# Adding the causal mask on VectorE inside the maximum instead of on TensorE, in a two-layer transformer kernel

## What is computed

```
scores = q @ k.T * scale                     # 1024 x 1024 for each of 16 heads
scores[query, key] = -inf  where key > query # causal
probs  = softmax(scores)                     # subtracts the maximum of each query's row
y      = probs @ v
```

## Time and profile before

| | |
|---|---|
| median of 3 runs | 812.42 us |
| the three runs | 810.61, 815.0, 812.42 us |
| span of the profiled execution | 814.8 us (the only time listed for that execution; it is 0.2 us under the slowest of the three) |
| attention of layer 0, maxima and scores | about 36 to 180 us of the span |
| attention of layer 1, maxima and scores | about 463 to 607 us |

### The profile page before, as it was taken

One profiled execution on the slowest core, in us unless ns is written; L12 is line 12 of the kernel. 1 busy time (PEld: TensorE's weight loads), 2 busy tenths in 40 slices (PEclk: granted clock), 3 DMA queues, 4 the chain that ended last, 5 costly groups with the idle time before them and its releaser, 6 DMA issues.

```text
span 814.8 us, 13117 instructions
## 1 busy us (share of the span) xinstructions
PE 667.2 (82%) x4319; PEld 434.2 (53%) x4319; DVE 475.5 (58%) x1293; ACT 331.5 (41%) x693; POOL 241.8 (30%) x276
## 2 busy tenths in 40 slices
PE   3979999993878999999506879999982999999960
PEld 2534344332547999999404424334331646899950
DVE  4498788427773344444395798778317662234457
ACT  3554566672233333222124444576763231333301
POOL 2140101210026775444300470101210003477620
PEclk9998999997689999999856989999997599999995
DMA  3442210320139999998340533030006100299662
GB/s 93 142 134 88 73 33 1 121 87 1 52 118 300 315 315 305 310 303 287 132 140 1 155 118 104 3 109 2 2 2 219 62 0 27 88 285 310 214 206 72
DMA packets 60325, 108.52 MB, mean 133 GB/s; under 512 B 11237, under 2 KB 37179, under 8 KB 60132
## 3 DMA queue, kind: packets, MB, share of 16 engines
q1 hardware_dynamic: 52564, 93.86, 35.9%
q0 software_dynamic: 7632, 13.80, 5.3%
q10 hardware_dynamic: 64, 0.03, 0.0%
HBM read 79.98 MB, written 19.79 MB: 122 GB/s over the span
## 4 chain that ended last, share of the span: by engine, by line
PE 62%; DVE 24%; ACT 4%; DMA 4%; issue 3%; SPq 1%; POOL 1%; ACTq 0%; POOLq 0%; DVEq 0%
PE ps L1023 15%; DVE mx L1411 9%; PE ps L838 7%; PE ps L822 6%; PE ps L793 5%; PE ps L911 5%; PE ps L1036 5%; PE ps L1038 5%; DVE X L1720 3%; PE ps L753 2%; PE ps L737 2%; ACT X L1164 2%; PE ps L880 2%; PE ps L997 2%; PE ps L982 1%
## 5 line engine op out<-in xcount | busy, mean ns | idle before, releaser
L1411 DVE TENSOR_REDUCE mx<-ps 128x1 f32<-128x512 f32 (+3 forms) x304 | 180.3, 656 | 44.4 <-PE ps L796 37.3
L1164 ACT ACTIVATE X<-ps 128x1024 f32<-128x1024 f32 (+1 forms) x192 | 146.3, 810 | 78.0 <-PE ps L822 77.4
L793 PE MATMUL ps<-KA,QA 112*128 112x512 bf16 (+3 forms) x384 | 113.2, 344 | 8.1 <-DMA KA<-X 2.7
L702 POOL DMA_INDIRECT outs<-X,token x95 | 94.9, 999 | 72.8 <-DVE X L1698 56.3
L694 POOL DMA_INDIRECT V<-token_rows,row_of_slot x64 | 65.4, 1021 | 123.7 <-DVE row_of_slot L1595 63.2
L672 POOL TENSOR_SCALAR_AFFINE_SELECT X<-X 128x512 f32<-128x512 f32 x64 | 40.8, 638 | 203.1 <-ACT X L1164 203.1
L1023 PE MATMUL ps<-QA,KA 128*128 x756 | 95.2, 276 | 4.5 <-ACT QA L1256 3.7
L822 PE MATMUL ps<-QA,KA 114*128 114x512 bf16 (+3 forms) x384 | 93.2, 329 | 4.5 <-ACT X L1164 3.4
L1023 PEld LDWEIGHTS ps<-QA,KA 128*128 128x128 f32 x756 | 91.9, 192 | 7.5 <-issue 5.6
L1685 DVE TENSOR_TENSOR X<-ps,X 128x128 f32<-128x128 f32 x95 | 27.7, 292 | 106.7 <-ACT X L1267 106.5
L838 PE MATMUL ps<-X,V 128*32 128x512 f32 (+3 forms) x768 | 81.1, 497 | 0.5 <-ACT X L1172 0.4
(11 more groups left out here) (255 smaller groups left out, 892.3 us busy)
## 6 DMA issues: line engine op xcount, KB each, us to landing
KA<-in_ex SPq DMA_DIRECT2D x95, 512.0 KB
X<-in_dn SPq DMA_DIRECT2D x95, 64.0 KB
outs<-empty SPq DMA_DIRECT2D x4, 1024.0 KB, 8.5
X<-outs SPq DMA_DIRECT2D x8, 512.0 KB, 6.3
V<-outs SPq DMA_DIRECT2D x8, 512.0 KB, 7.8
QA<-X SPq DMA_DIRECT2D x28, 128.0 KB, 2.4
KA<-X SPq DMA_DIRECT2D x28, 128.0 KB, 2.5
QA<-w_sdn SPq DMA_DIRECT2D x28, 128.0 KB, 2.5
```

The costliest lines, as they stand in the source:

```text
L702: pool.indirect_dma_start(out=outs[L], out_offset=bass.IndirectOffsetOnAxis(ap=token[L][:, i:i + 1], axis=0), in_=erows[:, g % OUT_RING, : ...
L793: mm = pe.matmul(ps[:, bank, j * w:(j + 1) * w], QA[0:KQ, h, i * P:(i + 1) * P], KA[0:KQ, h, s0:s0 + w], start=True, stop=not diag)
L1164: nc.scalar.activation(probs[:, st % PB, 2 * p:2 * p + 2, off:CH], ps[:, 4 + 2 * p:6 + 2 * p, off:CH], ACT.Exp, scale=SCALE).then_inc(S(f" ...
L1411: v.tensor_reduce(mx[:, part, i, h0:h0 + nh], ps[:, n % RB, 0:nh * w].rearrange("p (h w) -> p h w", h=nh), AX.X, ALU.max)\
```

## The change

In units that hold one head and lie on the diagonal, TensorE no longer adds the mask. VectorE takes the maximum there with another instruction: it adds a mask row to the bank, element by element, writes the sums back over the bank, and gives the largest of them, at least -1e30, to `mx`. The mask becomes 512 columns wide (`mask_row`), 0 except for its last 128 columns, which are the former `mask_q`; the instruction takes its last 384 or 512 columns. Units with two or four heads a bank keep their matmul with the mask and their reduction. The order of the work and the semaphores stay.

```diff
-        mask_q = sb("mask_q", [P, P], BF16)
+        mask_row = sb("mask_row", [P, CH], BF16)
+        mask_q = mask_row[:, CH - P:CH]
...
-            for t in (identf, identb, mask_q):
+            for t in (identf, identb, mask_row):
                 ch.step(pool.memset(t[:, :], 0.0))
...
-            ch.step(pool.affine_select(out=mask_q[:, :], in_=mask_q[:, :], compare_op=ALU.is_ge, fill=-BIG,
+            ch.step(pool.affine_select(out=mask_q, in_=mask_q, compare_op=ALU.is_ge, fill=-BIG,
                                        base=0, pattern=[[-1, P]], channel_multiplier=1))
...
                             h = HG * g + h0 + j
-                            diag = s0 + w == (i + 1) * P
+                            diag = s0 + w == (i + 1) * P and nh > 1
                             mm = pe.matmul(ps[:, bank, j * w:(j + 1) * w], QA[0:KQ, h, i * P:(i + 1) * P],
                                            KA[0:KQ, h, s0:s0 + w], start=True, stop=not diag)
                             if diag:
-                                mm = pe.matmul(ps[:, bank, (j + 1) * w - P:(j + 1) * w], identb[:, :], mask_q[:, :],
+                                mm = pe.matmul(ps[:, bank, (j + 1) * w - P:(j + 1) * w], identb[:, :], mask_q,
                                                start=False, stop=True)
...
-                        v.tensor_reduce(mx[:, part, i, h0:h0 + nh],
-                                        ps[:, n % RB, 0:nh * w].rearrange("p (h w) -> p h w", h=nh), AX.X, ALU.max)\
-                         .then_inc(S(f"unit_out{L}"), 1)
+                        if nh == 1 and part == 1:
+                            ins = v.tensor_tensor_reduce(ps[:, n % RB, 0:w], ps[:, n % RB, 0:w], mask_row[:, CH - w:CH], 1.0, -BIG,
+                                                         ALU.add, ALU.max, mx[:, part, i, h0:h0 + 1])
+                        else:
+                            ins = v.tensor_reduce(mx[:, part, i, h0:h0 + nh],
+                                                  ps[:, n % RB, 0:nh * w].rearrange("p (h w) -> p h w", h=nh), AX.X, ALU.max)
+                        ins.then_inc(S(f"unit_out{L}"), 1)
```

## The result

| | before | after |
|---|---|---|
| median | 813.48 us (14 executions, 809.46 to 817.4) | 817.33 us (14 executions, 815.02 to 820.17) |
| ratio | | 1.005, 95% interval 1.0031 to 1.007 |
| span of the profiled execution | 814.8 us | 817.6 us |
| attention of layer 0, first maximum to last negation | 115.57 us | 117.19 us |
| the same, layer 1 | 115.28 us | 116.73 us |

The kernel became slower by 3.9 us (2.5 to 5.7 by the interval), where 5.1 more were predicted. The 817.5 us of the forecast came closer, because it started from 812.42, the median of the first three executions; that of all 14 is 813.48. The profiled pair differs by 2.8 us in span and by 1.62 + 1.45 = 3.07 us in the two attention stages, so in this pair the expert stages have no part in the loss.

The account below looks back on a forecast made before the run. VectorE's full runs of maxima were taken to bound the early attention groups, TensorE's saving counting only before waits. 2.70 us a layer, less 0.26 in layer 0, made +5.1: 812.4 + 5.1 = 817.5 us, range 809.5 to 829.

Parts of the forecast that it names:

- The direction and the place: Attention stages: slower by 5.1 us, from VectorE's full runs, mainly in groups 0 and 1; elsewhere waits absorb part.
- Two instructions for one: Each of 128 changed units: a main VectorE instruction near 0.69 us plus a small second one that reads the maximum.
- The rival in which the maximum costs nothing: Changed VectorE units: only 0.007 us added each, so -2.7 us in all and 809.7 us; chance 0.20.
- D: Extra VectorE time per changed unit, for second input, write to PSUM and maximum: 0.087 us, with ends at 0.007 and 0.25.
- The second input and the write over the bank at 7 ns: Main VectorE instruction of each changed unit: 690 ns against 683 for the reduction, nothing more for writing PSUM.
- The rival of a stream at half rate: Changed units: reading and writing one bank halves VectorE's rate, about +59 us, 871 us; chance 0.05.
- The read-out at 0.08: Second small VectorE instruction of each changed unit: 0.08 us, taken from a pair of small independent instructions.
- The saving on TensorE: 128 mask matmuls of 0.06 us go, 7.7 us at most; worth something only before VectorE's waits, nothing inside its runs.
- The sum: Per layer 0.70 + 0.28 + 0.81 + 0.91 = 2.70 us; two layers, less 0.26 in layer 0, +5.1 us.
- Its explanation of the clock: TensorE's longer waits for VectorE's negated maxima could lower its clock to 1.2 GHz more often; range leaned up 1 to 2 us.
- Its signs: Second small row, 0.69 us between starts, mask matmuls 256 to 128, attention stages +2.6 us each; a 0.5 clock meant wrong.
- TensorE as the bound: Groups 2 and 3 and mixed stretches: all 128 masks come off the path, 7.7 us, giving 804.7 us; chance 0.05.

Follow-up runs that it names:

- masks twice: Kernel after, but TensorE also adds its mask in the 128 changed units as before: 816.47 us, ratio to the kernel before 1.0034.
- the four kernels of low clock: No mask in the 128 units, all sums to SBUF, early units only, and the kernel after: mean clocks 0.916, 0.916, 0.914, and 0.915 and 0.913.
- block 6 alone: New instruction only in the 32 units of query block 6, the rest as in the kernel before: 847.58 us against 849.98, ratio 0.9963.
- the early runs alone: New instruction only in group 0 and the first half of group 1 (48 units), the rest as in the kernel before: 817.59 us, ratio 1.0047.

## Why the prediction was right, point by point

- **The direction and the place: right.** The long early runs are VectorE's. With the same wait in front, the first half of group 1 grows from 7.69 to 8.11, +0.42 = 8 x 0.046 + 0.05. In groups 2 and 3 the waits and the saved masks pay.
- **Two instructions for one: right.** The "Trainium skill", page "VectorE: DVE Perf Modes", section "Two Vector instructions with no wait between them", says that an operation that writes out its accumulator is a main instruction and a read; the trace agrees, with 128 read-outs of 0.14 us. The rival in which the maximum costs nothing is out in its mechanism. In its price it was near with sums in SBUF: D = 0.01.
- **The second input and the write over the bank at 7 ns: right**, nothing was measured (0.60 us apart). The rival of a stream at half rate is out.
- **The read-out at 0.08: too high.** It is 0.046. The row from which it was taken, the pair at 6.87 and 6.95, is of two small instructions; behind a long one, even an ordinary small one costs 0.06. The lower row, 0.05 us between the parts of the index search, would have been the better choice. The 0.05 us at the end of each run was missed.
- **The saving on TensorE: right** in the steady groups. By the prediction's formula such a group changes by 12D - 0.59; at D = 0, 0.008 and 0.045 that is -0.59, -0.49 and -0.05, and these were measured. At D = 0.087 it was to be +0.46.
- **The sum: near in its total, partly for the wrong reason, and so by luck.** With D = 0.046 and 0.05 for the tail, a layer gives 0.42 + 0.04 + 0.42 - 0.01 - 0.10 = 0.77 us; two layers, less 0.26 in layer 0, give 1.3 us and not 5.1. The stages grew by 3.07 us in one profiled pair and by 2.09 in the other, and the medians by 3.9 and 2.9. Part of the gap lies in the sum's other terms: where the clock did not reach across, the second half of group 1 grew from 18.88 to 19.04 us (+0.16, not -0.01) and that of group 0 in layer 0 from 18.40 to 18.57 (+0.17, not +0.04). Another part is the clock, to which the prediction gave "1 to 2 us" at the top of its range and no term: the 0.6 us above came on top in one stage more of each pair. How the 3.9 and 2.9 of the medians split beyond that is not shown. A term too large and others too small or left out came near the same total.
- **Its explanation of the clock was half of it.** It named longer waits of TensorE for VectorE. But with masks twice VectorE is just as late, and the clock stayed at 0.922: less work on TensorE early in the stage is what the four kernels of low clock share. That this is the cause is inferred from that grouping; no run gave TensorE other work in place of the masks.
- **Its signs.** The second small row, the fall of the mask matmuls from 256 to 128 and the growth of both attention stages were seen. The size was not: 0.65 us between starts and not 0.69, and 1.6 and 1.5 us a stage and not 2.6. The clock of 0.50 where it had been near 1, named as a sign of being wrong in kind, was seen as well (68 to 71 us).
- **TensorE as the bound: out.** With the masks gone and no D the kernel gained 2.3 us of 7.7. By the same formulas with D = 0 it should be 2 x (-0.24 - 0.24 - 1.18) = -3.3; the missing 1 us is within the interval. Layer 1 of its profile, where the clock at 0.50 reached into the second half of group 1, points the same way: that half was 0.87 us longer than before.

## What to carry to other kernels

Price an accumulating VectorE instruction as two, and send its elementwise result to SBUF where it isn't needed: 0.01 us a unit instead of 0.046 was the difference between a loss and none here. Make the trade only for units in front of which or behind which the loaded engine waits anyway: block 6 alone gained 0.4%, the early runs alone lost 0.5%. And look at the granted clock over many executions, on one chip, when work is taken off TensorE near a long wait: on these chips it was lower where that had been done, and one profile shows only one of its values.

A version with only the late units and the sums in SBUF was not tried.

## What was not expected of the hardware

- The read-out of the accumulator lasts 0.14 us when the elementwise output goes to PSUM and 0.08 us when it goes to SBUF, with starts 0.65 and 0.61 us apart for 512 columns. The destination of the maximum is the same in both.
- VectorE adds a bf16 row from SBUF to a bank and writes it back over the same bank at the pace of a reduction, 0.60 us for 512 columns.
- Executions of one kernel differ in where the stretch at 1.2 GHz lies after the same wait: the kernel after had it from 61.1 to 71.3 us in one profile and from 62.9 to 69.7 in the other, and the first half of group 1 took 8.93 and 8.26 us.
